# A graph network on one core: GpSimd waits for the landing of each pair of gather groups before it issues the next pair

## What is computed

```python
def rgcn_conv(x, src, dst, etype, W, root, bias):
    n = x.shape[0]
    seg = dst * R + etype
    x_src = x[src]
    agg = jax.ops.segment_sum(x_src, seg, num_segments=n * R)
    cnt = jax.ops.segment_sum(jnp.ones((src.shape[0],), x.dtype), seg, num_segments=n * R)
    agg = jnp.where(cnt[:, None] > 0, agg / jnp.maximum(cnt, 1.0)[:, None], 0.0)
    agg = agg.reshape(n, R, -1)
    return jnp.einsum('nrd,rdk->nk', agg, W) + x @ root + bias
...
h = jnp.concatenate([x, node_emb[node_type]], axis=-1)
h = jax.nn.relu(rgcn_conv(h, src, dst, edge_type, W1, root1, b1))
h = jax.nn.relu(rgcn_conv(h, src, dst, edge_type, W2, root2, b2))
h = rgcn_conv(h, src, dst, edge_type, W3, root3, b3)
```

## Time and profile before

| what | value |
|---|---|
| runs | 7019.02, 7025.52, 7033.47 us (median 7025.52) |
| span of the profiled execution (the only time that is given of it) | 7027.7 us |
| busy: PE, DVE, POOL | 4925.6, 2875.6, 3636.8 us |
| POOL's gathers for convolutions 0 and 2 (2552), busy | 2653.3 us |
| POOL's gathers for convolution 1 (940), busy | 899.5 us |
| first gather of convolution 0, 1, 2 starts at | 1488.1, 4142.67, 5573.27 us |

### The profile page before, as it was taken

The page is one execution under the profiler, slowest core; times in us unless marked ns, Lnnn a source line. Parts: engine busy times, 40 slices in busy tenths (PEclk is TensorE's granted clock), DMA queues, the critical chain, the costliest instruction groups (busy, mean ns, idle before and its releaser), DMA issues.

```text
span 7027.7 us, 95103 instructions
## 1 busy us (share of the span) xinstructions
PE 4925.6 (70%) x35932; PEld 3076.0 (44%) x35932; DVE 2875.6 (41%) x8139; ACT 1023.1 (15%) x2385; POOL 3636.8 (52%) x3575
## 2 busy tenths in 40 slices
PE   2776789955655655656554448888888788888887
PEld 1544556633333333333333334444444445544544
DVE  5766661136666666666662211111112212111212
ACT  2544440002222222212220000000000000000000
POOL 4000000036666666666666646666666566666664
PEclk6888889977777777777776669999999899999999
DMA  2222216543434434434343334554545444444443
GB/s 77 96 111 100 90 64 227 219 135 113 121 106 120 120 105 122 119 112 117 114 116 97 97 116 134 168 167 148 169 137 167 154 138 146 138 139 147 142 135 104
DMA packets 428468, 904.12 MB, mean 129 GB/s; under 512 B 71170, under 2 KB 335116, under 8 KB 406124
## 3 DMA queue, kind: packets, MB, share of 16 engines
q0 software_dynamic: 169216, 348.44, 18.4%
q1 hardware_dynamic: 129028, 454.04, 17.7%
q10 hardware_dynamic: 129768, 95.53, 4.3%
HBM read 692.22 MB, written 205.05 MB: 128 GB/s over the span
## 4 chain that ended last, share of the span: by engine, by line
PE 43%; another core or an unknown queue 15%; issue 9%; DVE 8%; ACT 2%; DVEq 1%; DMA 0%; SPq 0%; ACTq 0%; POOL 0%; POOLq 0%
PE bank L1450 23%; PE bank L1408 7%; PE bank L1428 5%; PE bank L1495 2%; PE bank L1473 2%; PE bank L1412 2%; ACT stage L1558 1%; DVE stage L1560 1%; DVE scaled L1730 1%; DVE rel_hot L1679 1%; DVE type_scaled L1730 1%; DVE lo_dense_hot L1678 1%; DVE sums L1691 1%; DVE sums L1737 1%
## 5 line engine op out<-in xcount | busy, mean ns | idle before, releaser
L1395 POOL DMA_INDIRECT messages<-table,src_rows x2552 | 2653.3, 1040 | 1384.9 <-issue 692.0
L1450 PE MATMUL bank<-slices,pieces 128*128 128x384 fp8e4 x10290 | 1978.4, 337 | 375.5 <-issue 361.2
L1450 PEld LDWEIGHTS bank<-slices,pieces 128*128 128x128 bf16 x10290 | 988.8, 100 | 1211.6 <-issue 704.5
L1428 PE MATMUL bank<-rel_hot,lo_dense_hot 128*128 128x240 bf16 (+1 forms) x2688 | 589.2, 331 | 914.5 <-ACT stage L1558 463.2
L1395 POOL DMA_INDIRECT messages<-table,rel_rows x940 | 899.5, 957 | 560.8 <-issue 250.7
L1691 DVE TENSOR_TENSOR sums<-sums,bank 128x120 f32 x873 | 236.4, 271 | 2292.1 <-remote 1826.1
L1408 PE MATMUL bank<-group_hot,messages 128*128 128x120 bf16 x10476 | 832.5, 239 | 238.8 <-issue 112.8
L1408 PEld LDWEIGHTS bank<-group_hot,messages 128*128 128x128 bf16 x10476 | 747.4, 111 | 357.1 <-issue 204.8
L1428 PEld LDWEIGHTS bank<-rel_hot,lo_dense_hot 128*128 128x128 bf16 x2688 | 193.0, 106 | 1243.6 <-ACT stage L1558 532.2
L1377 POOL IOTA iota_rel_i<- 128x490 int32 x1 | 1.4, 1394 | 1355.2 <-DMA table<-typed_rows 1355.2
L1558 ACT CAST stage<-bank 128x500 fp8e4<-128x500 f32 x672 | 387.2, 576 | 1772.5 <-PE bank L1428 1094.9
(11 more groups left out here) (251 smaller groups left out, 3593.3 us busy)
## 6 DMA issues: line engine op xcount, KB each, us to landing
slices<-relations_d SPq DMA_DIRECT2D x70, 1200.0 KB
slices<-relations_d SPq DMA_DIRECT2D x70, 1152.0 KB
adjacency_d<-adjacency SPq DMA_DIRECT2D x15, 4704.0 KB, 14.5
adjacency<-adjacency_d SPq DMA_DIRECT2D x15, 4704.0 KB, 15.0
relations_d<-stage ACTq DMA_DIRECT2D x84, 500.0 KB
messages<-table,src_rows POOLq DMA_INDIRECT x2552
relations_d<-stage ACTq DMA_DIRECT2D x84, 480.0 KB
inverse<-inverse_d SPq DMA_DIRECT2D x52, 640.0 KB
```

The lines of the kernel that those rows point to most:

```text
L1395: pool.indirect_dma_start(messages[:, i % MESSAGES, t, 0:ROWS[v]], None, GATHERED[v], bass.IndirectOffsetOnAxis(ap=rows[:, e:e + 1], axis= ...
L1428: mm = pe.matmul(bank[REL_BANKS[n]][:, q * width:(q + 1) * width], lo_dense_hot[:, b % 2, m + q, :], hot, start=True, stop=True)
L1450: mm = pe.matmul(bank[DENSE_BANKS[K % 2]][:, 0:CHUNK], pieces[M % PIECE_RING][:, tile % PIECE_TILES, piece * P:(piece + 1) * P], slice_of_ ...
```

## The change

`conv_pool` gets one wait more. At each even group of a convolution from its third group on, before the group's four gathers are issued, POOL waits until the gathers of the group before have landed (64 more on that slot's semaphore). Two groups are issued without this wait, then comes the wait, then the next two. The wait on `group_psum` stays as it was, and every other engine's program is the same.

```diff
 MESSAGES = 6
+BURST = 2
...
                 for g in range(PLANS[v].groups):
                     i = GROUPS_BEFORE[v] + g
                     if i >= MESSAGES:
                         pool.wait_ge(group_psum, i - MESSAGES + 1)
+                    if g >= BURST and g % BURST == 0:
+                        pool.wait_ge(gathered[(i - 1) % MESSAGES], 16 * GROUP * ((i - 1) // MESSAGES + 1))
                     for t in range(GROUP):
```

## The result

The changed kernel takes 7251.57 us (median of 4 runs, 7235.59 to 7268.63), the kernel before, run beside it, 7026.92 us. The ratio is 1.0321, with a 95% interval of 1.0303 to 1.0338: slower by 225 us, where 62 us were forecast. The profiled execution took 7268.63 us with a span of 7266.7 us, which is 239.0 us above the span before.

What follows compares the result with a forecast made beforehand. It took POOL's landing waits, slightly over break-even, to become the bound: stretches longer by 120 us, less 58 us given back, make +62 us on the 7025.5 us median, 7087.5 us; range 7015 to 7205 us.

Steps and rivals of the forecast that it cites:

- The two heaps: Sign of being right: POOL's 435 idle times before gathers gather near 1.8 us and above 4 us.
- The break-even: Mean pause per pair above which POOL becomes the bound: 2.07, 2.06 and 2.11 us in convolutions 0, 1 and 2.
- the price of a pause: POOL's wait for a pair's landing, read from TensorE's waits: 1.83 us quiet, 4.5 us beside loads.
- The quiet pause: Landing wait with no load beside it, from a weight load in TensorE that awaited a fourth group's last gather: 1.83 us.
- the forecast's three means: Mean pauses mixed from quiet and loaded prices: 2.23, 2.52 and 2.40 us in convolutions 0, 1 and 2.
- A second term: Share of pairs ending beside a load, at 4.5 us each: 14.8%, 25.7% and 21.4% in convolutions 0, 1 and 2.
- Given back: TensorE's lead at the ends of the three convolutions shrinks to the last gather's landing, so 58 us come back.
- TensorE's 4.21 us per group: TensorE's pace at convolution 1's end once POOL is silent, against 5.92 us over the stretch; claimed TensorE can follow.
- No change: Rival, chance 0.20: mean landing under or near 2.07 us, so the existing 2.13 us pause hides the new one; 7025 us.
- Faster: Rival, chance 0.10: gathers hold TensorE back and enforced pauses free it, making pauses 1.83 us; up to 108 us, 6971 us.
- Far slower: Rival, chance 0.10: slot pauses at odd groups and landing pauses at even ones add up; about 7580 us, half 7335.
- The fixed cost of about 2.0 us plus bytes: Rule beside the forecast: every gather's landing takes 2.2 us, some 60 us, all given back at the ends; no change.

Runs made afterwards that it cites:

- The swap: The changed kernel with the two waits of a pair's first gather in the other order, the landing first: 7117.28 us, 1.0115 of the kernel before.

## Why the prediction was right and wrong

**Right.** The sign, and the way it came: POOL's stop at each pair, its length against 2.07 us, POOL as the new bound, a lead of 1.8 us at the end of convolutions 1 and 2 (within 5 us was named), no stop at odd groups. The two heaps were there too, the lower at 2.4 us where 1.8 was named. The break-even is sound where stops are replaced one for one: 117 x (2.84 - 2.06) = 91 us plus 8 us of longer gathers are convolution 1's 99; 117 x (2.69 - 2.11) = 68, plus 3 of gathers and 14 of longer gaps are the 85 of convolution 2. In convolution 0, 201 x (2.82 - 2.07) = 151 us, plus 20 of gaps, less 64, since the gathers took 1674.54 us in place of 1738.84: 107. Why they were shorter there is open.

**The step that failed** is the price of a pause: "I take TensorE's reaction to the semaphore, which is in these numbers, for POOL's." The quiet pause was 1.83 us from a weight load; POOL's is 2.4. At the one landing shown that both await, TensorE starts 0.15 us sooner than POOL (1514.30 and 1514.45), and the wait standing ahead of a gather with a wait of its own costs another 0.48. On the forecast's three means that is 0.59, 0.32 and 0.29 us, and 201 x 0.59 + 117 x 0.32 + 117 x 0.29 = 190 us. The swap shows the separate instruction to be the cause of most of it: with it out of the way the pauses are 165 us shorter. What is left of a quiet pause is 1.98 us (median, in convolution 0), near the 1.83 of the forecast. A second term was off the other way: a landing more than 3 us after the last gather, which the forecast puts down to a load beside it, came at 14% of the pairs of convolution 0, as forecast, but at 13% and 9% in convolutions 1 and 2, where 25.7% and 21.4% were taken. That hid part of the error there.

So it is in part luck that the swapped kernel's stretches grow by 119 us where 120 were forecast: its pauses by themselves make 201 x 0.31 + 117 x 0.43 + 117 x 0.26 = 143 us, and shorter gathers in convolution 0 take 46 of them off again, with some 20 us of longer gaps and gathers on the other side.

**Given back**: 58 forecast, 50 measured. In the swapped kernel, whose pauses were near the forecast, it was 26, since POOL was not the bound at every pair and TensorE kept a lead of 11.7 to 13.6 us. So with stretches that grew as forecast, 93 us were lost where the forecast had 62.

**A premise that other kernels refute.** The forecast says of a mean pause that "one below it leaves the bound where it is", and that with loaded pauses rarer "the change costs nothing", as long as TensorE keeps its pace. It does not keep it: landing waits at every fourth group keep POOL's own sum under the old stretch (1337 against 1391.5 us in convolution 1 by that run's expectation), and the stretch still lasted 1455.7 us. The forecast took TensorE's 4.21 us per group, read where POOL is silent, as a sign that TensorE can follow; beside gathers it keeps that pace only as long as POOL's stops allow.

**The rivals.** *No change* needed a mean pause under 2.07 us: the quiet ones alone were 2.4, and with the swap the means were still 2.37 to 2.49. *Faster* saw rightly that TensorE's results are late while gathers are under way; half the gathers show it plainly. And the enforced stops do free TensorE: its waits for nothing before dense matmuls fall from 361.2 to 37.4 us in the changed kernel. It brings no time, since each enforced stop costs POOL 2.7 to 2.8 us where its own cost 2.1, and POOL is then the bound. *Far slower* did not happen: POOL stops at even groups only. The fixed cost of about 2.0 us plus bytes that the Trainium skill gives ("DMA: Bandwidth & Descriptors", section on the anatomy of one DMA on the SWDGE path), and by which nothing was lost, is near what this trace shows: the landing comes a median 1.7 us after the last gather of a pair ends, 2.65 us after it starts. That formula has no term for what POOL needs from the landing to the next gather, 0.26 or 0.74 us here.

## What to carry to other kernels

Before you price a wait, see which instruction will carry it: of two waits ahead of one instruction the later written one was separate here, so the wait that ends last belongs first in the code. Take the price from the same engine, with its restart in it. And where an engine shares a stretch with one that stops at intervals, ask what the other engine does in these stops: a stop may be no slack for that other engine, and one that replaces it is only free if it is as short.

## What the runs showed of the hardware

- A gather that itself carries the late wait starts 0.26 us after the landing; behind a separate waiting instruction 0.74 us. A separate wait that is satisfied long before costs nothing (gaps of 0.30 us, 1.0006).
- POOL's indirect gathers hold up TensorE: 3 to 9 us after POOL has resumed, sooner where the matmuls are narrow, TensorE begins to start them by ones to fours, at steps of 0.71 us, until POOL stops for about 2 us; it gets through some 70 matmuls per stop. The signals of finished groups come late too (median 2.9 us in convolution 1, 0.14 us with a stop at every group). Neither a quarter of the bytes, nor a slot less, nor one twelfth of the columns changes it; half the gathers, or all of them with a stop at every group, remove it.
- What the two engines share there is not shown, and stays open, as does why stops for slots lengthen to some 2.4 us where landing waits stand at every fourth group. Instruction fetch, a rival that no run tests, has 289 packets on its larger queue in the span of the kernel before, one per 24 us, where POOL stops about every 12 us in convolution 1.
- No version that does the whole computation was faster than the kernel before by more than can be told.
